# Cross-attention to 257 keys: scores waited for and signalled in halves, and another order of ScalarE's copies

## The reference

```python
q = (layernorm(x) @ Wq.T).reshape(B, SQ, 16, 8)          # B 128, SQ 32
kv = (context @ Wkv.T).reshape(B, 257, 2, 16, 8)
att = softmax(einsum('bxhd,byhd->bhxy', q, k) * 8 ** -0.5, axis=-1)
x = x + einsum('bhxy,byhd->bxhd', att, v).reshape(B, SQ, 128) @ Wout.T + bout
```

## Time and profile before

| what | value |
|---|---|
| median of 3 runs | 3991.93 us (3991.15 to 3996.01) |
| the profiled execution | 3982.57 us, its span 3980.8 us |
| granted share of TensorE's clock over the span | 0.925, in the three cross-attentions 1.00 |
| busy in the span | PE 85%, PEld 62%, DVE 67%, ACT 59%, POOL 61% |
| exponentials of `a_cross`, first to last start | 20.2 to 505.2 us |
| of `e_cross` | 2147.3 to 2632.8 us |
| of `t_cross` | 2889.7 to 3375.9 us |

### The profile page before, as it was taken

The page is one execution under the profiler, slowest core; times in us unless marked ns, Lnnn a source line. Parts: engine busy times, 40 slices in busy tenths (PEclk is TensorE's granted clock), DMA queues, the critical chain, the costliest instruction groups (busy, mean ns, idle before and its releaser), DMA issues. The chain is left out here.

```text
span 3980.8 us, 119953 instructions
## 1 busy us (share of the span) xinstructions
PE 3385.2 (85%) x44674; PEld 2469.3 (62%) x44674; DVE 2670.8 (67%) x7002; ACT 2362.3 (59%) x6308; POOL 2422.3 (61%) x2724
## 2 busy tenths in 40 slices
PE   7999959999999579698698999978499999786866
PEld 5777737777777467365466777745277777453444
DVE  6888757777777523477445888857778887754655
ACT  6777736666666334386124777745577777644633
POOL 6767656776777343574425887746367676845733
PEclk9999979999999689898799999989599999887968
DMA  2111110000000122101221111110011111000023
GB/s 75 36 42 36 36 70 6 8 11 11 8 6 2 63 72 77 47 14 47 67 72 59 51 45 42 37 60 4 17 37 36 42 36 30 3 2 6 2 93 94
DMA packets 90549, 149.05 MB, mean 37 GB/s; under 512 B 10112, under 2 KB 66816, under 8 KB 89664
## 3 DMA queue, kind: packets, MB, share of 16 engines
q1 hardware_dynamic: 79936, 122.87, 9.9%
q0 software_dynamic: 10240, 20.99, 1.7%
HBM read 112.76 MB, written 31.06 MB: 36 GB/s over the span
## 5 line engine op out<-in xcount | busy, mean ns | idle before, releaser
L2251 POOL TENSOR_TENSOR t_cross_E<-t_cross_E,t_cross_inverse 128x1028 f32<-128x1028 f32 x128 | 243.2, 1900 | 134.8 <-DVE t_cross_inverse L2530 134.8
L2251 POOL TENSOR_TENSOR a_cross_E<-a_cross_E,a_cross_inverse 128x1028 f32<-128x1028 f32 x128 | 243.2, 1900 | 132.8 <-DVE a_cross_inverse L2530 132.8
L2477 ACT ACTIVATE t_cross_E<-t_cross_psum,t_cross_negtop 128x257 f32<-128x257 f32 x512 | 238.8, 472 | 113.5 <-DVE t_cross_negtop L2520 110.0
L2477 ACT ACTIVATE a_cross_E<-a_cross_psum,a_cross_negtop 128x257 f32<-128x257 f32 x512 | 238.8, 472 | 112.4 <-DVE a_cross_negtop L2520 103.9
L2477 ACT ACTIVATE e_cross_E<-e_cross_psum,e_cross_negtop 128x257 f32<-128x257 f32 x512 | 238.8, 472 | 111.2 <-DVE e_cross_negtop L2520 103.3
L2251 POOL TENSOR_TENSOR e_cross_E<-e_cross_E,e_cross_inverse 128x1028 f32<-128x1028 f32 x128 | 243.2, 1900 | 94.2 <-DVE e_cross_inverse L2530 94.1
L3090 PEld LDWEIGHTS l_psum<-l_ffn_w,l_hidden 128*128 128x128 f32 x1536 | 197.9, 192 | 98.0 <-issue 56.1
L3090 PE MATMUL l_psum<-l_ffn_w,l_hidden 128*128 128x128 f32 x1536 | 207.8, 278 | 19.0 <-POOL l_hidden L2963 17.9
L3083 PE MATMUL l_psum<-l_hT,l_ffn_w 128*128 128x512 f32 x384 | 200.6, 625 | 0.9 <-ACT l_hT L3139 0.9
L2520 DVE TENSOR_REDUCE t_cross_negtop<-t_cross_psum 128x2 f32<-128x514 f32 x256 | 175.8, 687 | 32.6 <-PE t_cross_psum L2337 31.7
L2520 DVE TENSOR_REDUCE a_cross_negtop<-a_cross_psum 128x2 f32<-128x514 f32 x256 | 175.4, 686 | 26.8 <-PE a_cross_psum L2332 26.4
(11 more groups left out here) (754 smaller groups left out, 11124.1 us busy)
## 6 DMA issues: line engine op xcount, KB each, us to landing
a_cross_context<-context SPq DMA_DIRECT2D x32, 578.0 KB, 3.7
e_cross_context<-context SPq DMA_DIRECT2D x32, 578.0 KB, 3.7
t_cross_context<-context SPq DMA_DIRECT2D x32, 578.0 KB, 3.7
u_moe_weights<-pack_u_moe SPq DMA_DIRECT2D x1, 5633.0 KB, 16.3
slots<-l_blank SPq DMA_DIRECT2D x6, 832.0 KB, 12.2
a_moe_x_slots<-slots SPq DMA_DIRECT2D x26, 192.0 KB, 2.8
slots<-a_moe_y_slots SPq DMA_DIRECT2D x26, 192.0 KB, 2.1
c_moe_x_slots<-slots SPq DMA_DIRECT2D x26, 192.0 KB, 2.8
```

The lines of the kernel that those rows point to most:

```text
L2251: pool.tensor_tensor(E[:, n % N], E[:, n % N], spread(inverse[:, n % 4], SK, 2), ALU.mult).then_inc(s_unit, 1)
L2477: act.activation(E[:, n % N, g], psum[:, g, 0:SK], ACT.Exp, bias=negtop[:, n % 2, g:g + 1], accum_out=total[:, n % 2, g:g + 1]).then_inc(s ...
```

## The change

Three edits, all in `cross_attention`:

- PE's `scores` goes in two halves of two groups each. Half 0 waits until two exponentials of the batch before are done, half 1 until four are, and each half raises `s_score` by one when done. In `t_cross` a half's two mask matmuls follow its two score matmuls.
- DVE's `maximum` waits for its own half.
- ACT's step begins with `second_half(n-3)`, ahead of `begin` and `values_out`.

```diff
-                if exists(i, n - 1):
-                    pe.wait_ge(s_exp, (i * N + n) * G)
-                for g in range(G):
...
-                last.then_inc(s_score, 1)
+                for half in range(2):
+                    if exists(i, n - 1):
+                        pe.wait_ge(s_exp, (i * N + n - 1) * G + 2 * half + 2)
+                    for g in (2 * half, 2 * half + 1):
                         rows = slice(g * 32, (g + 1) * 32)
+                        last = pe.matmul(psum[:, g, 0:SK], q_heads[rows, n // 4 % 2, n % 4].rearrange("p j s -> p (j s)"),
+                                         kT[rows, n % 2], start=True, stop=mask is None)
+                    if mask is not None:
+                        for g in (2 * half, 2 * half + 1):
...
+                    last.then_inc(s_score, 1)
...
             def step(i, n):
+                if exists(i, n - 3):
+                    second_half(i, n - 3)
                 begin(i, n - 1)
                 if exists(i, n):
                     values_out(i, n)
-                if exists(i, n - 3):
-                    second_half(i, n - 3)
                 side_out(i, n - 1)
...
             def maximum(i, n, half):
-                if half == 0:
-                    dve.wait_ge(s_score, i * N + n + 1)
+                dve.wait_ge(s_score, (i * N + n) * 2 + half + 1)
```

More of the change, by code:

```diff
@@ L2327, in scores @@
                     pe.wait_ge(s_heads, i * 2 + n // 4 + 1)
-                if exists(i, n - 1):
-                    pe.wait_ge(s_exp, (i * N + n) * G)
-                for g in range(G):
[L2331 to L2335, removed]
-                        rows = slice(g * 32, (g + 1) * 32)
-                        last = pe.matmul(psum[:, g, 0:SK], fold_bf[rows].rearrange("p j s -> p (j s)"), mask_neg[rows],
-                                         start=False, stop=True)
-                last.then_inc(s_score, 1)
+                for half in range(2):
+                    if exists(i, n - 1):
+                        pe.wait_ge(s_exp, (i * N + n - 1) * G + 2 * half + 2)
+                    for g in (2 * half, 2 * half + 1):
+                        rows = slice(g * 32, (g + 1) * 32)
+                        last = pe.matmul(psum[:, g, 0:SK], q_heads[rows, n // 4 % 2, n % 4].rearrange("p j s -> p (j s)"),
+                                         kT[rows, n % 2], start=True, stop=mask is None)
+                    if mask is not None:
+                        for g in (2 * half, 2 * half + 1):
+                            rows = slice(g * 32, (g + 1) * 32)
+                            last = pe.matmul(psum[:, g, 0:SK], fold_bf[rows].rearrange("p j s -> p (j s)"), mask_neg[rows],
+                                             start=False, stop=True)
+                    last.then_inc(s_score, 1)
             def side(i, n):
```

## The result

The changed kernel takes 4068.72 us (median of 4, 4067.25 to 4070.74) against 3991.54 us for the kernel before beside it: a ratio of 1.019, 95% interval 1.0174 to 1.0206, or 77 us more. The forecast was 91 us more, a median of 4083.

The account below looks back on a forecast made before the run. Not PE but two chains, through bank 4 and through DVE's queue, end the steps. 29.2 us each in a_cross and e_cross and 32.4 in t_cross make +91 on 3991.9: 4083 us, range 4025 to 4145.

Parts of the forecast that it names:

- What ends a step: In the attentions' steps: two chains, through bank 4 and through DVE's in-order queue, end them; PE has about 0.26 us to spare.
- The chain through bank 4: From second_half's copy through PE's keys, kT, second maximum and third exponential to the next step; n = 1 takes 3.76 us.
- The halves at nothing: Scores in two halves: nothing gained or lost; price between 0 and 0.71 us a step, taken as 0.
- second_half first, keys at +0.84: ScalarE's second_half at T0 frees bank 4 early, keys start at +0.84, and n = 1 gains 0.17 us.
- 0.48 us of delay of the other copies: values_out and begin, now behind second_half, start 0.48 us later, and DVE work that waits for them moves as much.
- The steps: Lengths forecast in us: n = 0 4.14, n = 1, 5 3.59, n = 2, 6 4.12, n = 3, 7 4.45, n = 4 3.82.
- The sum: Three attentions together: 91 us more, so 3991.9 becomes 4083 us.
- over 127 steps: 0.23 us more a step over 127 steps: 29.2 us each in a_cross and e_cross; t_cross at 0.255 a step, 32.4 us.
- Much slower: Rival: the halves' row groups don't overlap on PE, up to 0.71 us more a step, 4163 us; chance 0.09.
- Faster: Rival: only bank 4's chain counts, DVE has room before the first maximum; 46 us less, 3946 us; chance 0.05.
- No change: Rival: the copies' delay is about half, n = 1's gain comes in more steps, both cancel; about 3992 us; chance 0.04.
- PE's busy time stays: In the profile after, PE's busy time stays as it is, with more idle between.

Follow-up runs that it names:

- e1: Score halves and their waits as in the change, ScalarE's copy order as before; ratio 1.0007 to the kernel before, a turn of 30.47 us.
- e6: Kernel before, whole scores, with second_half first only in steps with n % 4 = 1; ratio 0.9960 to the kernel before.
- e9: Changed kernel, second_half first only at n % 4 = 1, second maximum ahead of the next keys only at n % 4 = 0; ratio 0.9940 to the kernel before.
- e10: Kernel before, whole scores, second_half first only at n % 4 = 1, second maximum ahead of keys only at n % 4 = 0; ratio 0.9956 to the kernel before.
- e7: Halves signalled apart but issued back to back after all four exponentials, ScalarE's order as before; one run 4005.4 us, kernel before 4001.2 to 4011.9.
- e4: Changed kernel, but E_last, output and v_last read an SBUF constant and don't wait for values_out; one run 4003.3 us, a turn of 30.57.

## Why the prediction was right, point by point

- *What ends a step.* Right. The chain through bank 4 ended n = 1, and shortening it gave 0.19 us there; the chain through ScalarE's first copy and VectorE's queue was the path in n = 3 and 7. By the forecast's own lengths it had 0.04 us of room in n = 0, 0.12 in n = 2 and 0.42 in n = 4, so a delay of 0.48 put it on the path there.
- *The halves at nothing.* Right within some 2 us an attention, by e1 and e6: the waits more that were taken at nothing cost 0.03 us a turn in `a_cross` and 0.12 in `t_cross`, all of it in n = 0. This holds for the order that VectorE has; with the second maximum ahead of the keys (e9, e10) the early half shortens n = 4.
- *second_half first, keys at +0.84.* They start at +0.79, so n = 1 gains 0.19 and not 0.17.
- *0.48 us of delay of the other copies.* Measured 0.477 at the median, and 0.48 for each of VectorE's waits.
- *The steps.* Off by 0.03 us at most except n = 6 (4.02, forecast 4.12). I had taken n = 6 like n = 2 without reading it. In the kernel before its reciprocal starts at +0.85, and n = 2's at +0.92; the difference is VectorE's loop, for with the loop written out both steps take 4.00. n = 2 itself came out 0.03 shorter, kT following the maximum after 0.58 and not 0.60.
- *The sum.* Forecast 91 us, measured 72 in the attentions. The term that was mis-sized is "over 127 steps". A looped turn of `a_cross` cost 1.69 us more and not 1.84. The first turn cost 0.81, the second 1.39, the 13 in the middle 21.9 and the last 1.13, in sum 25.2 and not 29.2; the first and the last have other work or no loop, and the first varies by itself (before the change its n = 1 takes 3.67 us in `a_cross` and 4.85 in `t_cross`). `e_cross` is lower yet, since nine of its turns are written out. The other 5 us of the 77 need no cause in the change. Outside the attentions the profiled execution after is 12 us longer than the one before, 2536.6 against 2524.1, but with the halves alone, whose attentions are as long as before, it is 2538.2. Without the attentions the code of all these kernels is the same, and the execution before was the quickest there.
- *Much slower.* Fell by the result and with e7. *Faster* fell because the room ahead of kT is only the 0.12 that was named; e4, which makes that room, has the short steps that this rival asked for. *No change* fell too.
- *PE's busy time stays.* Wrong, though nothing hung on it. It is 487.23 us now, where the earlier trace rows have 452.58:

```profile
20.00:529.00 509.00, 487.23 (x5110) 358.43 (x5108) 377.11 (x910) 370.67 (x1360) 337.31 (x341) 1.00 0.12 36
213.99 1.19 PE L2333 MATMUL a_cross_psum<-a_cross_kT,a_cross_q_heads 32*128 32x257 f32 x8
```

The first line is the windows view of the changed kernel, the second PE's timeline in n = 1. The same eight passes cover 1.19 us instead of 0.71 because half 0 starts 0.33 us before T0 and half 1 at +0.16. The scores alone (the windows view with --source L2332, then L2333) are 90.91 us before and 117.05 after, so they are 26 of the 35 us. With the order alone PE is at 468.62 of 511 us, the scores at 91.99; no run here takes this other part apart. PE has no more work, and the busy share of 96% reads as if it were the bound.

## What to carry to other kernels

Before a copy is moved ahead of another on an in-order engine, list who waits for the one that is moved back, and what stands behind that wait on its engine; here three small operations on a tile carried 0.48 us into the main chain of three steps in four. Several chains of nearly the same length can end a loop's steps in turn, so an order that is right for one step is wrong for its neighbour, and it can be chosen by step. A signal that comes earlier is worth nothing until the work that it releases is the last thing awaited.

## What the runs showed of the hardware

- Copies on ScalarE begin before the last one has ended: behind the 128x512 copy of 0.59 to 0.60 us the next starts 0.476 us later, behind the 128x256 one (0.38) 0.264 later, and behind the 128x128 one of aT (0.27) 0.157 later. The distance, and not the duration, is what moving a copy costs.
- Matmuls on different groups of 32 rows aren't held to the order of issue: 0.72 us for the scores of four groups, with the mask of two of them issued in between (e7).
- A loop on VectorE costs 0.44 to 0.49 us a turn where nothing hides it, 0.37 of the 0.48 in `a_cross` in the first step of a turn.
